# Eight feed-forward jobs turned in 32x32 blocks on VectorE and by way of DRAM, with the first layer's later layer norms moved to earlier steps

## What is computed

```python
x = x + 0.5 * ffn(_layernorm(x), W_fc, W_proj)
x = x + attn(_layernorm(x), ...)       # running sums along the tokens
x = x + 0.5 * ffn(_layernorm(x), W_fc, W_proj)

def ffn(x, W_fc, W_proj):
    h = jnp.square(jax.nn.relu(jnp.einsum('bsd,fd->bsf', x, W_fc)))   # 128 -> 512
    y = jnp.einsum('bsf,df->bsd', h, W_proj)                          # 512 -> 128
    ...   # five steps with a threshold: the number of spikes / 5

def attn(x, ...):
    h = _layer_norm(x, gamma, beta)
    keys, values = h @ Wk.T + bk, h @ Wv.T + bv
    w = jnp.exp((keys @ Wka.T + bka) / sqrt(128))
    return jnp.cumsum(w / jnp.cumsum(w, axis=1) * keys, axis=1) * values
```

## Time and profile before

| | |
|---|---|
| median of 3 runs | 148.12 us (147.59 to 148.47) |
| the profiled execution | 147.76 us |
| its span, first to last instruction | 146.0 us |
| TensorE busy | 140.3 us (96%) |
| VectorE busy | 117.3 us (80%) |
| ScalarE busy | 113.8 us (78%) |
| GpSimd busy | 95.8 us (66%) |
| TensorE transposes of `normed` into `work` | 62 seen, 9.4 us busy |

### The profile page before, as it was taken

One profiled execution on the slowest core, in us unless ns is written; L12 is line 12 of the kernel. 1 busy time (PEld: TensorE's weight loads), 2 busy tenths in 40 slices (PEclk: granted clock), 3 DMA queues, 4 the chain that ended last, 5 costly groups with the idle time before them and its releaser, 6 DMA issues.

```text
span 146.0 us, 2901 instructions
## 1 busy us (share of the span) xinstructions
PE 140.3 (96%) x945; PEld 126.1 (86%) x945; DVE 117.3 (80%) x403; ACT 113.8 (78%) x215; POOL 95.8 (66%) x141
## 2 busy tenths in 40 slices
PE   7899999999999999999999999999999999999990
PEld 7689898989989899998988989889789898979790
DVE  3894559388699989999779999999999978453674
ACT  3278877789896996959979697796796977977761
POOL 1439247929999929894998989989967952520300
PEclk9999999999999999999999999999999999999999
DMA  4975000000000000000000000020020102020222
GB/s 140 270 203 161 4 2 0 0 0 4 2 0 2 0 4 2 0 0 0 4 0 0 0 0 7 0 72 0 2 76 0 57 15 72 7 72 0 72 72 72
DMA packets 10510, 5.09 MB, mean 35 GB/s; under 512 B 1152, under 2 KB 10496, under 8 KB 10496
## 3 DMA queue, kind: packets, MB, share of 16 engines
q1 hardware_dynamic: 9808, 4.53, 10.7%
q10 hardware_dynamic: 688, 0.39, 0.9%
HBM read 2.82 MB, written 2.10 MB: 34 GB/s over the span
## 4 chain that ended last, share of the span: by engine, by line
PE 48%; DVE 25%; issue 14%; POOL 6%; DMA 3%; POOLq 1%; ACT 1%; ACTq 1%; DVEq 0%
PE work L932 19%; PE hidden L853 5%; PE hidden L857 5%; PE hidden L854 5%; POOL normed L386 4%; DMA proj_raw<-in_L_ffn_W_proj_dram 3%; DVE weight_sum L699 3%; PE work L866 2%; POOL rstd L380 2%; DVE stats L559 2%; DVE pooled L723 2%; DVE share_bank L713 2%; DVE weight_key L706 2%; DVE share_bank L718 2%; DVE stats_att L559 2%
## 5 line engine op out<-in xcount | busy, mean ns | idle before, releaser
L932 PE MATMUL work<-proj_t,square 128*128 128x128 f32 x480 | 61.2, 275 | 0.0
L932 PEld LDWEIGHTS work<-proj_t,square 128*128 128x128 f32 x480 | 58.8, 192 | 2.4 <-ACT square L460 0.4
L460 ACT ACTIVATE square<-relu 128x512 f32<-128x512 f32 x60 | 37.7, 641 | 0.7
L455 ACT ACTIVATE relu<-hidden 128x512 f32<-128x512 f32 x64 | 36.7, 606 | 0.1
L853 PE MATMUL hidden<-in_hi,fc_lo 128*128 128x512 f32 (+1 forms) x66 | 27.5, 417 | 0.1
L857 PE MATMUL hidden<-in_lo,fc_hi 128*128 128x512 f32 (+1 forms) x66 | 25.6, 387 | 0.0
L854 PE MATMUL hidden<-in_hi,fc_hi 128*128 128x512 f32 (+1 forms) x66 | 25.4, 385 | 0.0
L380 POOL TENSOR_TENSOR rstd<-var_eps,minus_half 128x4 f32<-128x4 f32 x15 | 15.2, 1012 | 14.7 <-DVE neg_mean L572 14.7
L632 DVE TENSOR_TENSOR in_lo<-work,in_hi 128x512 fp32r<-128x512 f32 x15 | 10.2, 680 | 12.3 <-ACT in_hi L451 12.3
L386 POOL TENSOR_SCALAR normed_att<-x_att,neg_mean_att,rstd_att 128x128 f32<-128x128 f32 x32 | 18.1, 578 | 0.8
L386 POOL TENSOR_SCALAR normed<-x_second,neg_mean,rstd 128x128 f32<-128x128 f32 x32 | 16.9, 540 | 0.8
(11 more groups left out here) (118 smaller groups left out, 245.8 us busy)
## 6 DMA issues: line engine op xcount, KB each, us to landing
x_first<-_attn_hidden_states_dram SPq DMA_DIRECT2D x7, 256.0 KB, 4.0
out_dram<-x_out SPq DMA_DIRECT2D x7, 256.0 KB, 2.2
out_dram<-x_out SPq DMA_DIRECT2D x4, 64.0 KB, 1.5
x_first<-_attn_hidden_states_dram ACTq DMA_DIRECT2D x1, 128.0 KB, 2.7
x_first<-_attn_hidden_states_dram SPq DMA_DIRECT2D x1, 128.0 KB, 2.4
fc_raw<-in_L_ffn_W_fc_dram SPq DMA_DIRECT2D x1, 128.0 KB, 2.8
fc_raw<-in_L_ffn_W_fc_dram ACTq DMA_DIRECT2D x1, 128.0 KB, 3.3
proj_raw<-in_L_ffn_W_proj_dram SPq DMA_DIRECT2D x1, 128.0 KB, 3.1
```

Of the source, the lines that this page charges most:

```text
L455: nc.scalar.activation(relu[j.lane][:, c, :], bank_of_hidden(j, c)[:], ACT.Relu).then_inc(relu_made[j.lane], 1)
L460: nc.scalar.activation(square[j.lane][:, c, :], relu[j.lane][:, c, :], ACT.Square).then_inc(squares_act[j.lane], 1)
L932: last = nc.tensor.matmul(work[j.lane][:, tokens], square[j.lane][:, c, tokens], proj_t[:, c, :], start=(c == 0 and t == 0), stop=(c == NC ...
```

## The change

Two things are changed.

Jobs 3 to 10 (`BLOCK_TURNED`) are no longer turned by TensorE. VectorE transposes each 32x32 block of `normed` with one instruction over 128x512 (`ff_block_turn`) into one of three `blocks` buffers. SP stores that to DRAM (`block_rows`, 256 KB), waits for the store, and loads it with four transfers of 64 KB, each onto 32 partitions, into one of three `block_turned` buffers. `in_hi` and `in_lo` of these jobs are made from `block_turned` in SBUF. The lane's next `normed` waits for the block turn instead of TensorE's turn.

`LAYER_NORM_STEP` now says in which of VectorE's steps a job's statistics and arguments are made. It was j-1 for job j. Now it is step 0 for jobs 1 and 2, step 1 for 3 and 4, step 2 for 5 and 6, step 5 for 7, step 6 for 8, step 7 for 9, step 8 for 10; jobs 11 to 15 stay at j-1. In a step with two jobs, both jobs' statistics come first and then both jobs' arguments. GpSimd's `normalise` moves with them, and the block turn is made near the end of the same VectorE step, ahead of `att_sum` and of the one-time work of steps 1 and 2.

```diff
+LAYER_NORM_STEP = [-1, 0, 0, 1, 1, 2, 2, 5, 6, 7, 8, 10, 11, 12, 13, 14]
+BLOCK_TURNED = [3, 4, 5, 6, 7, 8, 9, 10]
+QUARTER = 32
+BLOCK_SETS = 3
...
+def layer_norms(i):
+
+    return [FeedForward(k) for k in range(len(FF_JOBS)) if LAYER_NORM_STEP[k] == i]
...
+        def by_token(tile):
+
+            return tile[:].rearrange("p (a t j) -> p t a j", a=P // QUARTER, t=NT)
+
+        def in_quarters(tile):
+            return tile[:].rearrange("p (t a j) -> p t a j", a=P // QUARTER, t=NT)
...
+            for k, index in enumerate(BLOCK_TURNED):
+                j = FeedForward(index)
+                sp.wait_ge(blocks_made[j.lane], blocks_before(j) + 1)
+                sp.dma_start(block_rows[k].ap(), blocks[k % BLOCK_SETS][:]).then_inc(blocks_stored[k], 16)
+                sp.wait_ge(blocks_stored[k], 16)
+                quarters = block_rows[k].ap().rearrange("(a i) (b n) -> b i a n", i=QUARTER, b=P // QUARTER)
+                if k >= BLOCK_SETS:
+                    last = FeedForward(BLOCK_TURNED[k - BLOCK_SETS])
+                    sp.wait_ge(lo_made[last.lane], last.turn + 1)
+                for q in range(P // QUARTER):
+                    part = block_turned[k % BLOCK_SETS][q * QUARTER:(q + 1) * QUARTER, :]
+                    sp.dma_start(part.rearrange("p (a n) -> p a n", n=P),
+                                 quarters[q]).then_inc(blocks_loaded[k], 16)
...
-                if turn:
-                    pool.wait_ge(turned[kind], turn)
+                wait_read()
...
+            def wait_ff_read(j):
+                for last in feed_forward(j.index - 2):
+                    if last.by_blocks:
+                        pool.wait_ge(blocks_made[j.lane], blocks_before(j))
+                    else:
+                        pool.wait_ge(turned[j.lane], turned_before(j))
...
             for i in range(FIRST_STEP, STEPS):
-                for j in feed_forward(i + 2):
+                for j in layer_norms(i + 1):
                     ff_normalise(j)
...
+                if j.by_blocks:
+                    k = BLOCK_TURNED.index(j.index)
+                    act.wait_ge(blocks_loaded[k], 16 * (P // QUARTER))
+                    act.wait_ge(hidden_made[j.lane], NC * j.turn)
+                    nc.scalar.activation(in_quarters(in_hi[j.lane]), by_token(block_turned[k % BLOCK_SETS]),
+                                         ACT.Copy).then_inc(hi_made[j.lane], 1)
+                    return
...
+            def ff_block_turn(j):
+                if j.by_blocks:
+                    dve.wait_ge(normed_made[j.lane], NT * (j.turn + 1))
+                    k = BLOCK_TURNED.index(j.index)
+                    if k >= BLOCK_SETS:
+                        dve.wait_ge(blocks_stored[k - BLOCK_SETS], 16)
+                    rows = blocks[k % BLOCK_SETS]
+                    nc.vector.transpose(rows[:].rearrange("p (b t j) -> p t b j", b=P // QUARTER, t=NT),
+                                        normed[j.lane][:].rearrange("p t (b i) -> p t b i", i=QUARTER)
+                                        ).then_inc(blocks_made[j.lane], 1)
...
-                    else:
+                for j in layer_norms(i):
+                    if j.index > 0:
                         ff_layer_stats(j)
-                for j in feed_forward(i + 1):
+                for j in layer_norms(i):
                     if j.index > 0:
                         ff_layer_args(j)
...
+                for j in layer_norms(i):
+                    ff_block_turn(j)
                 for b in attention(i):
                     att_sum(b)
...
             def ff_turn(j):
-
+                if j.by_blocks:
+                    return
```

More of the change, by code:

```diff
@@ L60, in __init__ @@
         self.is_last = i == len(FF_JOBS) - 1
+        self.by_blocks = i in BLOCK_TURNED
         if self.is_last:
@@ L242, in macaron_kernel @@
         normed = {k: sb(f"normed_{k}", [P, NT, P]) for k in KINDS}
+        blocks = [sb(f"blocks{k}", [P, S]) for k in range(BLOCK_SETS)]
+        block_turned = [sb(f"block_turned{k}", [P, S]) for k in range(BLOCK_SETS)]
+        block_rows = [nc.dram_tensor(f"block_rows{k}", (P, S), F32) for k in range(len(BLOCK_TURNED))]
         in_hi = [sb(f"in_hi{l}", [P, S], F32R) for l in LANES]
@@ L290, in macaron_kernel @@
         turned, hi_made, lo_made = sems("turned", KINDS), sems("hi_made", KINDS), sems("lo_made", KINDS)
+        blocks_made = sems("blocks_made", LANES)
+        blocks_stored = [sem(f"blocks_stored{k}") for k in range(len(BLOCK_TURNED))]
+        blocks_loaded = [sem(f"blocks_loaded{k}") for k in range(len(BLOCK_TURNED))]
         hidden_made, relu_made = sems("hidden_made", LANES), sems("relu_made", LANES)
@@ L313, in wait_relu, with turned_before, blocks_before @@
             engine.wait_ge(relu_made[j.lane], NC * j.turn + c + 1)
+        def turned_before(j):
+            return j.before(lambda other: not other.by_blocks)
+        def blocks_before(j):
+            return j.before(lambda other: other.by_blocks)
+        def by_token(tile):
+            return tile[:].rearrange("p (a t j) -> p t a j", a=P // QUARTER, t=NT)
+        def in_quarters(tile):
+            return tile[:].rearrange("p (t a j) -> p t a j", a=P // QUARTER, t=NT)
         def bank_of_hidden(j, c):
@@ L376, in first_inverse_deviation, with normalise @@
                                         minus_half[:, HALF_TILES:NT], ALU.pow).then_inc(rstd_made[j.lane], 1)
-            def normalise(kind, turn, source):
+            def normalise(kind, turn, source, wait_read):
                 pool.wait_ge(ln_args_made[kind], 2 * (turn + 1))
@@ L387, in normalise, with wait_att_read @@
                                             rstd[kind][:, t:t + 1], ALU.add, ALU.mult).then_inc(normed_made[kind], 1)
+            def wait_ff_read(j):
[4 more added lines that the diff above has]
+                        pool.wait_ge(turned[j.lane], turned_before(j))
+            def wait_att_read(b):
+                if b:
+                    pool.wait_ge(turned["att"], b)
             def ff_normalise(j):
@@ L392, in ff_normalise @@
                 else:
-                    normalise(j.lane, j.turn, x_of[j.layer][j.batch])
+                    normalise(j.lane, j.turn, x_of[j.layer][j.batch], lambda: wait_ff_read(j))
             def att_normalise(b):
-                normalise("att", b, x_of["att"][b])
+                normalise("att", b, x_of["att"][b], lambda: wait_att_read(b))
             def ff_squares(j):
@@ L449, in ff_hi @@
                     return
-                act.wait_ge(turned[j.lane], j.turn + 1)
+                if j.by_blocks:
[5 more added lines that the diff above has]
+                    return
+                act.wait_ge(turned[j.lane], turned_before(j) + 1)
                 nc.scalar.activation(in_hi[j.lane][:], work[j.lane][:], ACT.Copy).then_inc(hi_made[j.lane], 1)
@@ L631, in ff_lo @@
                 dve.wait_ge(hi_made[j.lane], j.turn + 1)
+                if j.by_blocks:
+                    nc.vector.tensor_tensor(in_quarters(in_lo[j.lane]), by_token(block_turned[BLOCK_TURNED.index(j.index) % BLOCK_SETS]),
+                                            in_quarters(in_hi[j.lane]).bitcast(F32),
+                                            ALU.subtract).then_inc(lo_made[j.lane], 1)
+                    return
                 nc.vector.tensor_tensor(in_lo[j.lane][:], work[j.lane][:], in_hi[j.lane][:].bitcast(F32),
                                         ALU.subtract).then_inc(lo_made[j.lane], 1)
+            def ff_block_turn(j):
[8 more added lines that the diff above has]
+                                        ).then_inc(blocks_made[j.lane], 1)
             def att_part_lo(b):
@@ L928, in ff_contract @@
                     return
+                if j.by_blocks and c == 0:
+                    pe.wait_ge(stairs_made[j.lane], STAIRS_A_JOB * j.turn)
                 wait_square(j, c)
```

## The result

The changed kernel takes 160.32 us (160.15 to 160.45), the kernel before 147.88 us beside it (147.59 to 148.47): a ratio of 1.0835, 95% interval 1.0796 to 1.0875. Forecast were 155.6 us and 152.0 to 159.0. The direction is right, the time is 4.6 us above the forecast (profiled execution: 160.15 us, span 158.4) and outside the range.

What follows compares the result with a forecast made beforehand. TensorE was taken to bound the kernel, with VectorE right behind from step 9. The sum was 147.76 + 9.15 (stalls) - 0.86 (two turns) - 0.5 (steps 5 to 11) = 155.6 us, range 152.0 to 159.0.

Steps and rivals of the forecast that it cites:

- The wait of job 4's arguments for `normed` of job 2: Step 1, VectorE: job 4's arguments wait until `normed` of job 2 is made, delaying `in_lo` of job 1; +1.4 us.
- The chain of step 2: Job 4's block turn, waiting for `normed`, stands with fold and statistics ahead of `in_lo` of job 2; +4.8 us.
- GpSimd three deep: Step 3: GpSimd makes jobs 5 and 6 ahead of the first `normed_att`, delaying TensorE's matmuls; +2.65 us.
- the bound of 9.2: Worst-case round trip of a block-turned job through DRAM, 9.2 us, hidden under about 10 us.
- rival C: VectorE's block turn costs 1.2 us instead of 0.6, giving 158.6 us; chance 0.14.
- the 65.9: Time VectorE needs from the statistics of step 5 to those of step 12: 65.9 us.
- the lead into step 5: How far VectorE enters step 5 ahead of TensorE: some 1.8 us, instead of 1.33 before.
- lead out: How far VectorE is ahead of TensorE when leaving steps 5 to 11: 1.4 us, instead of 1.6 before.
- B: Rival: VectorE doesn't hold TensorE up in steps 5 to 11, giving 152.9 us; chance 0.13.
- D: Rival: TensorE's clock falls in the stall of step 2, adding up to 1.5 us, to 157.1; chance 0.07.
- E: Rival: moved layer norms fit into VectorE's idle time, no new stalls in steps 1 to 3, 143.8 us; chance 0.03.
- F: Rival: two of the forecast stalls overlap more than thought, giving 151 to 152 us; chance 0.05.

Runs made afterwards that it cites:

- experiment 4: Changed kernel with twenty added matmuls of `ones` on TensorE ahead of its wait for `in_lo` of job 2 in step 2; 160.6 us.
- Experiment 5: Changed kernel with only jobs 5 to 10 turned in blocks and the layer norms of jobs 1 to 4 back at j-1; 151.41 us.
- experiment 6: Changed kernel with VectorE's block turn of job 4 moved behind `in_lo` of job 2 in step 2; 157.18 us.
- Experiment 1: Changed kernel with `in_lo` of the eight block-turned jobs reading `work` in PSUM again instead of `block_turned` in SBUF; 157.52 us.
- experiment 7: Changed kernel with the edits of Experiment 5 and Experiment 1 together; 149.08 us, ratio 1.0079 to the kernel before.

## Why the prediction was right in direction and short by 4.6 us

**Steps 1 to 3: right, to 0.6 us.** The wait of job 4's arguments for `normed` of job 2 came (2.54 us), and its `in_lo` came 1.3 us late to TensorE (16.78 for 15.46), forecast 1.7. The chain of step 2 is as written: 4.79 us for 4.8, `in_lo` at 28.58, the matmul at 29.31, forecast 29.4. GpSimd three deep: the matmuls start at 38.00, forecast 37.75. The wait of 2 to 3 us ahead of them did not show as a wait, since the slow matmuls filled it; experiment 4 brings it out, 2.6 us. That the times agree to 0.25 us is partly luck: step 1 began 0.31 us earlier in this execution than in that of before (12.46 for 12.77), and counted from there the stalls come to 9.7 us and not 9.15. Experiment 5 removes both stalls together, experiment 6 the first.

**Transfers: right.** `in_hi` never waited for a load. Issues of the kernel after, KB and us to landing, answering:

```profile
block_rows<-blocks SPq DMA_DIRECT2D x8, 256.0 KB, 2.0
block_turned<-block_rows SPq DMA_DIRECT2D x32, 64.0 KB, 1.9
```

With issues of 0.34 and 0.43 us a round trip takes at most 5.6 us (2.0 from the store's issue to its landing, 1.7 for the four issues of the loads, 1.9 to the landing of the last), well under the bound of 9.2.

**The block turn: right enough.** 706 ns listed, 0.63 us until the next instruction starts (33.60 to 34.23); assumed 0.6. So rival C, and the estimate of 1.2 us from the Trainium skill ("VectorE: DVE Perf Modes", The three transpose paths), are not borne out for fp32 in one instruction over 128x512.

**The step that failed: "`in_hi` and `in_lo` of these jobs read SBUF instead of PSUM ... I cost that at nothing".** `in_hi` on ScalarE was right (615 ns). `in_lo` on VectorE was wrong. In steps 5 to 11 its six pieces took 7.22 us (1.50, 0.91, 0.67, 1.22, 1.43, 1.49) instead of 6 x 0.68 = 4.1: 3.1 us more, and VectorE's stretch was 3.0 over the 65.9. Experiment 1, which takes that cost away and nothing else, has 66.56 us for TensorE's steps 5 to 11 instead of 69.79: 3.2 of the 4.55 us by which the profiled execution missed are this term. The nearest row that I took, the same operation, had its first operand in PSUM, and the place of an operand decides here, not the work. The trace of before held a row that would have told it. VectorE and GpSimd share the last job's squares there, both operands of them in SBUF; VectorE's (count, then ns min/median/max) and GpSimd's:

```profile
L644 DVE TENSOR_TENSOR square<-relu x3: 680/693/1220, 130.8 to 139.0; 128x512 f32<-128x512 f32 x3
...
137.82 1.82 DVE L644 TENSOR_TENSOR square<-relu 128x512 f32<-128x512 f32 x2 [0.23 <-ACT relu L455]
...
137.39 1.11 POOL L401 TENSOR_TENSOR square<-relu 128x512 f32<-128x512 f32 x1 [8.91 <-ACT relu L455]
```

The first of the pair, at 137.82, is the long one: it ends at 139.04, 0.54 behind GpSimd's 138.50. The one at 130.8, with GpSimd idle, took 0.69.

**The second error: the lead into step 5.** The 1.8 us came out as 0.68 (53.68 less 53.00). It left out VectorE's waits for others in step 4:

```profile
46.15 0.83 DVE L694 TENSOR_TENSOR in_lo<-block_turned,in_hi 128x512 fp32r<-128x512 f32 x1 [1.26 <-ACT in_hi L508]
...
48.24 0.70 DVE L790 SCALAR_TENSOR_TENSOR share_bank<-share_bank,guess_share 128x512 f32<-128x512 f32 x1 [0.56 <-POOL guess_share L470]
```

The lead that VectorE would have gained by having less work went into these waits. That is 1.1 us, and 0.4 of it is the first error again: `guess_share` was late because it ran beside the `in_lo` at 46.15, and without that the lead was 1.10 (experiment 1). The other 0.7 is there in experiment 1 too, where the wait for `in_hi` is 1.28 us; that it alone makes up the 0.7 was not tested.

**The sum again.** 3.0 (stretch of VectorE) + 1.1 (lead in) + 0.15 (lead out, 1.55 and not 1.4) = 4.3 in steps 5 to 11, where TensorE takes 69.79 and not 65.5; with 0.25 in the steps before, 4.55: the profiled 160.15 less 155.6. By experiment 1 the place of `in_lo`'s operand is 3.2 of the 4.3, and 1.1 is the rest: 0.3 in the stretch, 0.7 in the lead, under 0.1 behind it. The turn of job 4 came off as forecast: 15.68 us from 38.00 to 53.68, before 16.11 (29.00 to 45.11).

**The rivals.** B had the bound wrong: in experiment 7, without the cost of `in_lo`, the stretch on VectorE is still 66.1 us. D's fall of the clock happened and cost 0.17 us between the two profiled executions, as the prediction's reason for a small price says; its 1.5 us was too much. E and F didn't occur. None of the rivals held the cost of `in_lo`, and the range gave it 0.1 us each way, which is why it was too narrow at the top. Without that cost the kernel takes 157.52 us, inside the range.
